# Splitting the MLP's operands into parts: three float32r products in place of one float32 product

## The chip, the core and the metric

The kernel is written directly for one core of a Trainium2 chip, whose engines run their own instruction queues and wait for each other by semaphores: TensorE (PE) for products and turns (transposes), VectorE (DVE), ScalarE (ACT), GpSimd (POOL), and SyncE (SP) for transfers. PE writes to eight banks of PSUM of 128 x 512 float32 values; the other data lie in SBUF. The metric is the time of one execution on the device, in microseconds (us), as the median of three runs.

## The reference

The input has 32 batches of 128 tokens with 128 channels. Two layers follow each other:

- layer 0 is a transformer block: modulated self-attention with 16 heads, cross-attention, and an MLP,
- layer 1 is a router over three experts with an evidence step and a gate.

The change concerns layer 0's MLP alone:

```python
x_norm2 = modulate(_ln(x), shift_m, scale_m)          # layer norm, then x * (1 + scale) + shift
h = jax.nn.gelu(x_norm2 @ W_mlp1 + b_mlp1)            # 128 -> 512
h = h @ W_mlp2 + b_mlp2                               # 512 -> 128
x = x + gate_m[:, None] * h
```

## The kernel before

Tokens are worked on in 8 groups (NG) of 4 batches (GB), 512 tokens (GT) each. The program has three stages.

**Attention**, rounds -1 to 7, by a table of steps with times (`round_steps`): each step is put at a time between 0 and 32 of its round, and every engine takes its own part of the steps in that order. Round 7 holds, beside the last attention, the derived weights of the router (`derive`), POOL's splitting of the router's weights into parts (`split`), and the first steps of the MLP. Round 8 (`i == NG`) mixes the last of attention with the MLP of groups 0 to 3.

**MLP.** The steps for a group g are:
- `stats` (DVE: statistics of the tokens, L806 to L812; POOL: add of epsilon and power, L648 and L650),
- `norm` (DVE: four operations, one for each batch, L820, from SBUF to SBUF),
- `xt` (PE: the tokens are turned so that channels are on partitions, L975),
- `xt_read` (ACT: modulation while reading the bank into `m_XT`, L725),
- `first` k = 0..3 (PE: product with a quarter of W_mlp1, L939) with the gelu of it on ACT (L713, into `m_H`); for k = 2 and 3 the gelu has a step `gelu` of its own,
- `second` k = 0..3 (PE: product with a quarter of W_mlp2, summed in one bank),
- `gate` (DVE, L835, reads that bank), `turn_back` (PE turns it back, DVE adds it to X, L841).

`MLP_STEPS` is the order of one round, each step with a lag: in the round of group i the engines do `stats` and `norm` of i + 2, `xt` of i + 1, `first` of i, `second` and `gate` of i - 1, `turn_back` of i - 2. Each engine takes its steps in this order and waits by semaphores for data and for free buffers. There is one `m_XT`, so `xt_read` of i + 1 stands behind the four `first` of i. Rounds 3 and 4 are a loop on the engines, the others are written out. From round 5 on (`rest_of_groups`) steps of the router's first groups are mixed in: the norm and turn of its tokens (`r_XN`), its scores (product with `KEYS`), the evidence (`r_EV`).

**Router**, all 8 groups, from about 405 us to the end. Its seven hidden products are already made of parts: POOL makes of a float32 tensor a part "high" in float32r (add of zero, L659) and a part "low" (the float32 tensor minus high, L661), and PE sums high x high, high x low and low x high in the bank. In the profile all products of MLP and router have the line of the helper that issues them, L939, and all turns L975.

## Time and profile before

| | |
|---|---|
| time, median of 3 runs | 579.82 us (578.67 to 581.12) |
| the profiled execution's own time | 578.05 us |
| its span | 576.3 us |
| busy: PE, DVE, ACT, POOL | 540.8, 424.9, 385.2, 271.3 us |
| granted TensorE clock over the span | 0.994 |

Busy times are those of one engine over the whole span and overlap each other. PE's weight loads (PEld) run beside its products. The MLP stage proper takes about 80 us of the span.

### The profile page before, as it was taken

How to read it: one execution, taken by the hardware profiler on the slowest of the kernel's cores; microseconds unless marked ns; L12 is line 12 of the kernel's file. 1: busy time of each engine (PE TensorE's matmuls, PEld its weight loads, DVE VectorE, ACT ScalarE, POOL GpSimd, SP SyncE). 2: the span in 40 equal slices, each digit the busy share in tenths (PEclk: the TensorE clock that was granted, in tenths of full speed). 3: DMA queues.
4: the chain of work that ended last, by engine and by line, in shares of the span. 5: the costliest groups of instructions: out<-in, count | busy, mean ns of one | idle time of the engine just before them, and what ended most of it. 6: DMA issues, size and time to landing. Idle time of an engine off the chain costs nothing.

```text
span 576.3 us, 16509 instructions
## 1 busy us (share of the span) xinstructions
PE 540.8 (94%) x6175; PEld 381.4 (66%) x6177; DVE 424.9 (74%) x1255; ACT 385.2 (67%) x897; POOL 271.3 (47%) x294
## 2 busy tenths in 40 slices
PE   7988998998999999999999889988999999999995
PEld 6745665666666666666667544444788788788895
DVE  4688987878899798899787445555586786786565
ACT  6548686777878778787777744564654854854862
POOL 5638669299494878888903110124034034034000
PEclk9999999899999999999999999999999999999998
DMA  4764656254143543334400010000001001000000
GB/s 130 162 173 127 175 155 164 56 122 126 52 116 89 134 115 97 105 90 115 114 5 3 2 36 0 2 1 19 0 19 40 18 20 36 18 18 20 19 20 18
DMA packets 48716, 39.38 MB, mean 68 GB/s; under 512 B 6241, under 2 KB 48002, under 8 KB 48642
## 3 DMA queue, kind: packets, MB, share of 16 engines
q1 hardware_dynamic: 46568, 34.62, 23.1%
q10 hardware_dynamic: 2074, 3.77, 2.3%
q8 instruction: 47, 0.77, 0.6%
q14 instruction: 27, 0.22, 0.1%
HBM read 10.06 MB, written 2.10 MB: 21 GB/s over the span
## 4 chain that ended last, share of the span: by engine, by line
PE 64%; DVE 12%; POOL 7%; DMA 5%; SPq 4%; issue 4%; ACT 3%; ACTq 0%; DVEq 0%; POOLq 0%
PE PS L939 35%; PE PS L1810 6%; PE PS L1776 5%; DVE NM L1592 3%; PE PS L975 3%; PE PS L1862 3%; SPq L1324 3%; PE PS L1874 2%; DMA Qs<-MT 2%; PE PS L1794 2%; PE PS L1832 2%; DMA Ks<-Kp 2%; PE PS L1867 2%; POOL rstd L1370 1%; POOL rest L1401 1%
## 5 line engine op out<-in xcount | busy, mean ns | idle before, releaser
L1592 DVE TENSOR_REDUCE NM<-PS 128x4 f32<-128x512 f32 x256 | 163.3, 681 | 30.8 <-PE PS L1776 30.2
L1478 ACT ACTIVATE PR<-PS 128x512 f32<-128x512 f32 x256 | 140.0, 601 | 27.1 <-PE PS L1794 26.5
L1776 PEld LDWEIGHTS PS<-Ks,Qs 64*128 64x128 bf16 x1024 | 57.0, 94 | 53.9 <-DVE NM L1592 29.3
L1776 PE MATMUL PS<-Ks,Qs 64*128 64x128 bf16 x1024 | 83.2, 218 | 6.4 <-DVE NM L1592 3.7
L1794 PE MATMUL PS<-Qs,Ks 64*128 64x128 bf16 x1024 | 83.6, 218 | 3.8 <-DMA Qs<-MT 3.2
L1810 PE MATMUL PS<-PR,Va 128*32 128x128 f32 x2048 | 82.9, 280 | 0.0
L733 ACT ACTIVATE r_HID<-PS,ANC 128x128 f32<-128x128 f32 x224 | 63.4, 383 | 20.2 <-PE PS L939 20.2
L648 POOL TENSOR_TENSOR m_veps<-m_mv,m_eps 128x4 f32<-128x4 f32 x16 | 3.2, 201 | 143.2 <-DVE m_mv L812 143.2
L1794 PEld LDWEIGHTS PS<-Qs,Ks 64*128 64x128 bf16 x1024 | 57.0, 94 | 7.4 <-DMA Qs<-MT 3.7
L1810 PEld LDWEIGHTS PS<-PR,Va 128*32 128x32 f32 x2048 | 48.3, 109 | 20.2 <-ACT PR L1478 6.1
L939 PE MATMUL PS<-r_NXS,r_WNS 128*128 128x512 f32 x168 | 53.1, 424 | 0.0
L939 PE MATMUL PS<-WO,r_HID 128*128 128x128 f32 x384 | 47.7, 278 | 0.5 <-DVE r_T L914 0.5
L939 PE MATMUL PS<-r_EVS,r_US 128*128 128x512 f32 x168 | 47.6, 392 | 0.0
L939 PEld LDWEIGHTS PS<-WO,r_HID 128*128 128x128 f32 x384 | 44.6, 192 | 2.0 <-DVE r_T L914 1.7
L1862 PE MATMUL PS<-XT,W 128*128 128x512 f32 x64 | 34.9, 633 | 1.9 <-ACT XT L1514 1.4
L939 PEld LDWEIGHTS PS<-r_EVS,r_US 128*128 128x128 f32 x168 | 31.5, 188 | 7.2
L713 ACT ACTIVATE m_H<-PS,V 128x512 f32<-128x512 f32 x32 | 21.4, 695 | 20.0 <-PE PS L939 20.0
L939 PEld LDWEIGHTS PS<-r_NXS,r_WNS 128*128 128x128 f32 x168 | 29.5, 189 | 7.8 <-issue 3.4
L939 PE MATMUL PS<-m_H,W 128*128 128x512 f32 x64 | 32.0, 600 | 2.5 <-DVE YT L835 2.5
L939 PE MATMUL PS<-m_XT,W 128*128 128x512 f32 x64 | 32.1, 601 | 0.3 <-ACT m_XT L725 0.3
L659 POOL TENSOR_TENSOR r_EVS<-r_EV,zeros 128x512 fp32r<-128x512 f32 x8 | 8.3, 1040 | 48.8 <-DVE r_EV L888 48.8
L762 ACT ACTIVATE r_GTH<-r_GS 128x512 f32<-128x512 f32 x8 | 5.1, 632 | 39.0 <-DVE r_GS L907 39.0
(197 smaller groups left out, 1102.3 us busy)
## 6 DMA issues: line engine op xcount, KB each, us to landing
Qs<-Qp SPq DMA_DIRECT2D x96, 128.0 KB
Ks<-Kp SPq DMA_DIRECT2D x90, 128.0 KB
CTXG<-in_ctx SPq DMA_DIRECT2D x8, 256.0 KB, 3.8
r_CTX<-in_ctx SPq DMA_DIRECT2D x8, 256.0 KB, 2.7
out<-X SPq DMA_DIRECT2D x8, 256.0 KB, 2.3
X<-in_x SPq DMA_DIRECT2D x7, 256.0 KB, 4.4
W<-in_weights ACTq DMA_DIRECT2D x2, 855.0 KB
Qs<-MT SPq DMA_DIRECT2D x62, 8.0 KB
```

Of the source, the lines that this page charges most:

```text
L713: nc.scalar.activation(H[:, k, :], FIRST_BANK[k % 2][:, :], ACT.Gelu_apprx_tanh, bias=vec("bmlp1", k))\
L733: last = nc.scalar.activation(HID[:, k, b * P:(b + 1) * P], HIDDEN_BANK[k % 3][:, b * P:(b + 1) * P], ACT.Silu, bias=ANC[:, k, bass.ds(g * ...
L939: return nc.tensor.matmul(to, lhsT, rhs, start=start, stop=stop)
L975: last = nc.tensor.transpose(bank[:, b * P:(b + 1) * P], source(b), ident[:, :])
L1324: sp.dma_start(to, source).then_inc(stacked[k], 16)
L1478: nc.scalar.activation(PR[:, u, :], T_BANK[u % 2][:, :], ACT.Exp, scale=SCALE)\
L1592: nc.vector.tensor_reduce(out=NM[:, c.b // 2, c.second, u // 2, u % 2 * 4:u % 2 * 4 + 4, 0], in_=S_BANK[score_bank(c, u)[0]][:, :].rearran ...
L1776: last = nc.tensor.matmul(S_BANK[bank][:, j * P:(j + 1) * P], Qs[c.stack][rows, lo + j, cols], Ks[c.stack][rows, lo + j, cols], start=True ...
L1794: last = nc.tensor.matmul(T_BANK[u % 2][:, j * P:(j + 1) * P], Ks[c.stack][rows, lo + j, cols], Qs[c.stack][rows, lo + j, cols], start=Tru ...
L1810: last = nc.tensor.matmul(O_BANK[p.turn][TW * j:TW * j + TW, at:at + P], Va[c.mem][:, c.b, 4 * (u // 2) + j, u % 2 * TW // 2:u % 2 * TW // ...
L1832: last = nc.tensor.transpose(O_BANK[c.turn][:, u * P:(u + 1) * P], OTs[:, u * P:(u + 1) * P], ident[:, :])
L1862: last = nc.tensor.matmul(PS[fill_bank(name, g)][:, :], w(WEIGHT[name[0]][kind]), source(name, g)[:, :], start=True, stop=True)
```

## The change

The products of the MLP are made as the router's are.

- The weights W_mlp1 and W_mlp2 are split by POOL in round 7 into `m_W1S` and `m_W2S`, two more `split` steps between those of the router's weights.
- The turned tokens: a new step `xt_parts` on DVE takes `m_XT` (ACT still writes it) and makes the high part (a copy that rounds to float32r) and the low part (a subtract) in one of two buffers `m_XTS0` and `m_XTS1`, by the group's parity. `xt_read` therefore waits for `xt_parts` of the group before in place of its `first`, and both stand right behind `xt` in the order.
- The gelu outputs: ACT makes the high part by a copy after each gelu (it waits for that gelu), POOL the low part by a subtract, in `m_HS`.
- Each `first` and `second` is three products of parts in float32r.
- The loop of rounds 3 and 4 is written out. The new tensors lie where attention's stacks `Qs` and `Ks` were, whose place in SBUF is moved for it. Semaphores of attention are used again.

```diff
@@ round_steps, i == NG - 1
-                 + [(t, "split", "weights", k, 0) for k, t in enumerate((2.5, 6.0, 22.5, 24.5))]
+                 + [(t, "split", "weights", k, 0) for k, t in enumerate((2.5, 6.0, 9.0, 12.0, 22.5, 24.5))]
@@ MLP_STEPS
-    ("stats", 2, 0), ("xt", 1, 0),
+    ("stats", 2, 0), ("xt", 1, 0), ("xt_read", 1, 0), ("xt_parts", 1, 0),
     ("first", 0, 0), ("second", -1, 0), ("first", 0, 1), ("second", -1, 1),
-    ("turn_back", -2, 0), ("norm", 2, 0), ("first", 0, 2), ("first", 0, 3), ("xt_read", 1, 0),
+    ("turn_back", -2, 0), ("norm", 2, 0), ("first", 0, 2), ("first", 0, 3),
     ("second", -1, 2), ("gelu", 0, 2), ("second", -1, 3), ("gelu", 0, 3), ("gate", -1, 0),
@@ gpsimd_programs, mlp
+            elif name == "first" and k < 2 or name == "gelu":
+                pool.wait_ge(h_high, 4 * g + (NG + k + 1))
+                nc.gpsimd.tensor_tensor(HS[:, 1, k, :], H[:, k, :], HS[:, 0, k, :], ALU.subtract).then_inc(h_split, 1)
@@ gpsimd_programs, split_weights
+            elif k in (2, 3):
+                pool.wait_ge(shifted_done, 16 * (2 * NG - 2))
+                to, source = ((W1S, w("mlp1")), (W2S, w("mlp2")))[k - 2]
+                return split(to, source, (weights_high, k + 1), weights_split)
@@ scalar_programs, gelu
             if later(g):
-                act.wait_ge(second_done, 4 * g + (k - 3))
+                act.wait_ge(h_split, 4 * g + (NG + k - 3))
             nc.scalar.activation(H[:, k, :], FIRST_BANK[k % 2][:, :], ACT.Gelu_apprx_tanh, bias=vec("bmlp1", k))\
                 .then_inc(gelu_done, 1)
+            act.wait_ge(gelu_done, 4 * g + (k + 1))
+            if later(g):
+                act.wait_ge(second_done, 4 * g + (k - 3))
+            nc.scalar.activation(HS[:, 0, k, :], H[:, k, :], ACT.Copy).then_inc(h_high, 1)
@@ scalar_programs, xt_read
-                    act.wait_ge(first_done, 4 * g)
+                    act.wait_ge(xt_split, g + NG)
@@ vector_programs, mlp
+            elif name == "xt_parts":
+                dve.wait_ge(xt_read, g + 1)
...
+                nc.vector.tensor_copy(XTS[par][:, 0, :], XT[:, :]).then_inc(xt_high, 1)
+                dve.wait_ge(xt_high, g + (NG + 1))
+                nc.vector.tensor_tensor(XTS[par][:, 1, :], XT[:, :], XTS[par][:, 0, :], ALU.subtract).then_inc(xt_split, 1)
@@ tensor_programs, mlp
-                product(FIRST_BANK[k % 2][:, :], w("mlp1", k * P, P), XT[:, :]).then_inc(first_done, 1)
+                chunk = slice(k * P, (k + 1) * P)
+                product(FIRST_BANK[k % 2][:, :], W1S[:, 0, chunk], XTS[par][:, 0, :], True, False)
+                product(FIRST_BANK[k % 2][:, :], W1S[:, 0, chunk], XTS[par][:, 1, :], False, False)
+                product(FIRST_BANK[k % 2][:, :], W1S[:, 1, chunk], XTS[par][:, 0, :], False, True).then_inc(first_done, 1)
...
-                pe.wait_ge(gelu_done, 4 * g + (k + 1))
-                product(SECOND_BANK[:, :], w("mlp2", k * P, P), H[:, k, :], start=k == 0, stop=k == 3)\
-                    .then_inc(second_done, 1)
+                pe.wait_ge(h_split, 4 * g + (NG + k + 1))
+                chunk = slice(k * P, (k + 1) * P)
+                product(SECOND_BANK[:, :], W2S[:, 0, chunk], HS[:, 0, k, :], k == 0, False)
+                product(SECOND_BANK[:, :], W2S[:, 0, chunk], HS[:, 1, k, :], False, False)
+                product(SECOND_BANK[:, :], W2S[:, 1, chunk], HS[:, 0, k, :], False, k == 3).then_inc(second_done, 1)
```

How this stands on the engines: first DVE in round 8, from the add of group 6's cross-attention result (L1725 before, L1766 after) to the statistics of group 3. `PS3` to `PS6` are PSUM banks, `rden` and `On` belong to attention, `m_XN` is the normalised tokens. Before:

```order
L1725 TENSOR_TENSOR X<-PS6,X 128x512
L820 TENSOR_SCALAR m_XN<-X,m_mv,m_rstd 128x128 x4
L806 BN_STATS m_stat<-X 128x6 x4
L810 COPY seen2<-m_stat 128x1
L812 BN_AGGR m_mv<-m_stat 128x2 x4
L1615 RECIPROCAL rden<-PS5 128x32
L1619 TENSOR_TENSOR On<-PS5,rden 128x256
L820 TENSOR_SCALAR m_XN<-X,m_mv,m_rstd 128x128 x4
```

After:

```order
L1766 TENSOR_TENSOR X<-PS6,X 128x512
L856 CAST m_XTS0<-m_XT 128x512
L858 TENSOR_TENSOR m_XTS0<-m_XT,m_XTS0 128x512
L839 TENSOR_SCALAR m_XN<-X,m_mv,m_rstd 128x128 x4
L825 BN_STATS m_stat<-X 128x6 x4
L829 COPY seen2<-m_stat 128x1
L831 BN_AGGR m_mv<-m_stat 128x2 x4
L1654 RECIPROCAL rden<-PS5 128x32
L1658 TENSOR_TENSOR On<-PS5,rden 128x256
L856 CAST m_XTS1<-m_XT 128x512
L858 TENSOR_TENSOR m_XTS1<-m_XT,m_XTS1 128x512
L839 TENSOR_SCALAR m_XN<-X,m_mv,m_rstd 128x128 x4
```

The parts of group 0 stand ahead of the norm of group 1, those of group 1 ahead of the norm of group 2.

Then POOL, where the router's first splits are mixed in. `m_veps` and `m_rstd` are its add and power, `r_NXS` and `r_EVS` the parts of the router's tokens and evidence. Before:

```order
L648 TENSOR_TENSOR m_veps<-m_mv,m_eps 128x4
L650 TENSOR_TENSOR m_rstd<-m_veps,half 128x4
L659 TENSOR_TENSOR r_NXS0<-r_NX0,zeros 128x512
L661 TENSOR_TENSOR r_NXS0<-r_NX0,r_NXS0 128x512
L648 TENSOR_TENSOR m_veps<-m_mv,m_eps 128x4
L650 TENSOR_TENSOR m_rstd<-m_veps,half 128x4
L659 TENSOR_TENSOR r_EVS0<-r_EV0,zeros 128x512
```

After:

```order
L655 TENSOR_TENSOR m_veps<-m_mv,m_eps 128x4
L657 TENSOR_TENSOR m_rstd<-m_veps,half 128x4
L664 TENSOR_TENSOR m_HS<-m_H,m_HS 128x512 x4
L669 TENSOR_TENSOR r_NXS0<-r_NX0,zeros 128x512
L671 TENSOR_TENSOR r_NXS0<-r_NX0,r_NXS0 128x512
L664 TENSOR_TENSOR m_HS<-m_H,m_HS 128x512 x4
L655 TENSOR_TENSOR m_veps<-m_mv,m_eps 128x4
L657 TENSOR_TENSOR m_rstd<-m_veps,half 128x4
L669 TENSOR_TENSOR r_EVS0<-r_EV0,zeros 128x512
```

Four subtracts of gelu outputs stand behind the router's first power, and four more behind its first split.

## Rows read from the trace of the kernel before

**Rows 1.** Page: busy time of each engine over the span

```profile
PE 540.8 (94%) x6175; PEld 381.4 (66%) x6177; DVE 424.9 (74%) x1255; ACT 385.2 (67%) x897; POOL 271.3 (47%) x294
```

**Rows 2.** Windows: stretch, its length, engines' busy us, clock, DMA

```profile
285.00:300.00 15.00, 14.35 (x283) 10.19 (x283) 12.58 (x27) 11.11 (x23) 2.30 (x3) 1.00 0.03 9
345.00:355.00 10.00, 10.00 (x32) 4.62 (x30) 5.53 (x22) 4.74 (x9) 1.21 (x2) 1.00 0.00 0
```

**Rows 3.** Timeline, round 3: start, us, engine, line, operation, count, idle

```profile
348.73 0.66 PE L975 MATMUL PS<-ident,m_XN 128*128 128x128 f32 x4
...
353.43 1.88 PE L939 MATMUL PS<-m_XT,W 128*128 128x512 f32 x4
...
355.15 1.88 PE L939 MATMUL PS<-m_H,W 128*128 128x512 f32 x4
...
357.07 0.66 PE L975 MATMUL PS<-ident,m_XN 128*128 128x128 f32 x4
357.24 1.36 DVE L835 TENSOR_SCALAR YT<-PS,mod,gbm 128x128 f32<-128x128 f32 x4 [1.77 <-PE PS L939]
...
359.49 0.37 DVE L812 BATCH_NORM_AGGREGATE m_mv<-m_stat 128x2 f32<-128x6 f32 x4
```

**Rows 4.** Timeline of PE in the router: two trios of float32r products

```profile
430.27 0.85 PE L939 MATMUL PS<-r_NXS,r_WNS 128*128 128x512 f32 x3
430.95 0.84 PE L939 MATMUL PS<-r_EVS,r_US 128*128 128x512 f32 x3
```

**Rows 5.** Groups from 300 us: line, operation, count, busy us, mean ns, idle

```profile
L713 ACT ACTIVATE m_H<-PS,V 128x512 f32<-128x512 f32 x32 | 21.4, 695 | 20.0 <-PE PS L939 20.0
L650 POOL TENSOR_TENSOR m_rstd<-m_veps,half 128x4 f32<-128x4 f32 x16 | 16.2, 1013 | 1.3
L725 ACT ACTIVATE m_XT<-PS,mod 128x128 f32<-128x128 f32 x32 | 12.1, 461 | 11.5 <-PE PS L939 11.5
L661 POOL TENSOR_TENSOR r_NXS<-r_NX,r_NXS 128x512 fp32r<-128x512 f32 x8 | 10.1, 1269 | 0.6
L884 DVE TENSOR_TENSOR r_WN<-r_E,r_rsum 128x512 f32<-128x512 f32 x8 | 5.5, 692 | 0.3
L762 ACT ACTIVATE r_GTH<-r_GS 128x512 f32<-128x512 f32 x8 | 5.1, 632 | 39.0 <-DVE r_GS L907 39.0
```

**Rows 6.** Timeline: norm of group 0 beside POOL, norm of group 1 alone

```profile
312.45 4.25 DVE L820 TENSOR_SCALAR m_XN<-X,m_mv,m_rstd 128x128 f32<-128x128 f32 x4 [1.42 <-POOL m_rstd L650]
...
313.50 1.27 POOL L661 TENSOR_TENSOR r_US<-U,r_US 128x512 fp32r<-128x512 f32 x1
314.72 0.82 POOL L659 TENSOR_TENSOR r_US<-U,zeros 128x384 fp32r<-128x384 f32 x1
315.63 1.00 POOL L661 TENSOR_TENSOR r_US<-U,r_US 128x384 fp32r<-128x384 f32 x1
...
322.50 1.11 DVE L820 TENSOR_SCALAR m_XN<-X,m_mv,m_rstd 128x128 f32<-128x128 f32 x4 [0.82 <-PE PS L975]
```

**Rows 7.** Timeline at the start: DVE and POOL subtract at once

```profile
15.69 1.22 POOL L1405 TENSOR_TENSOR Kp<-rest,Kp 128x512 bf16<-128x512 f32 x1
...
15.93 1.53 DVE L1717 TENSOR_TENSOR Qp<-rest,Qp 128x512 bf16<-128x512 f32 x1
```

**Rows 8.** Timeline: group 0's first products, and the turn of group 3

```profile
324.23 1.96 PE L939 MATMUL PS<-m_XT,W 128*128 128x512 f32 x4 [0.33 <-ACT m_XT L725]
...
340.66 0.63 PE L975 MATMUL PS<-ident,m_XN 128*128 128x128 f32 x4 [1.76 <-ACT m_XT L725]
```

**Rows 9.** Timeline: turn 7, router's first turn, scores, copy of evidence

```profile
374.91 0.60 PE L975 MATMUL PS<-ident,m_XN 128*128 128x128 f32 x4
...
380.08 0.60 PE L975 MATMUL PS<-ident,r_XN 128*128 128x128 f32 x4
...
383.10 1.06 PE L939 MATMUL PS<-KEYS,r_NX 128*128 128x131 f32 x8
...
395.87 0.69 DVE L888 COPY r_EV<-PS 128x512 f32<-128x512 f32 x1 [2.04 <-PE PS L939]
```

More of the change, by code:

```diff
@@ L258, in round_steps @@
                  + mlp_steps(8.43, "second", 0, 3) + mlp_steps(8.44, "norm", 3) + mlp_steps(8.45, "first", 1, 2)
-                 + mlp_steps(8.46, "first", 1, 3) + mlp_steps(8.47, "xt_read", 2) + mlp_steps(8.48, "gelu", 1, 2)
+                 + mlp_steps(8.46, "first", 1, 3) + mlp_steps(8.35, "xt_read", 2) + mlp_steps(8.36, "xt_parts", 2) + mlp_steps(5.11, "xt_parts", 1) + mlp_steps(8.48, "gelu", 1, 2)
                  + mlp_steps(8.49, "gelu", 1, 3) + mlp_steps(8.5, "gate", 0))
@@ L421, in rest_of_groups @@
         router(*step)
-    with eng.Fori(3, NG - 3) as i:
-        for name, lag, k in MLP_STEPS:
-            mlp(name, i + lag, k, 0, 0)
+    for i in range(3, NG - 3):
+        for step in valid_steps(MLP_STEPS, i):
+            mlp(*step)
     lead, second = valid_steps(ROUTER_STEPS, -2), valid_steps(ROUTER_STEPS, -1)
@@ L460, in mlp_and_router @@
 def mlp_and_router(nc, stack, X, V, ctxin, w, vec, rows1, condT, mod, gbm, half, zeros, YT, ident, PS, load_w2, out,
-                   bank_filled, bank_read, max_done, exp_done, o_normed, o_stored):
+                   bank_filled, bank_read, shifted_done, max_done, exp_done, o_normed, o_stored,
+                   high_ready, low_ready):
     def sb(name, shape, dt=F32):
@@ L532, in mlp_and_router @@
     D = rb("r_D", [P, GT])
+    W1S = rb("m_W1S", [P, 2, 4 * P], F32R)
+    W2S = rb("m_W2S", [P, 2, 4 * P], F32R)
+    XTS = [rb(f"m_XTS{k}", [P, 2, GT], F32R) for k in range(2)]
+    HS = rb("m_HS", [P, 2, 4, GT], F32R)
     reused.close()
@@ L555, in mlp_and_router @@
     bank_filled["mlp_xt"], bank_read["mlp_xt"] = xt_turned, xt_read
+    xt_high, xt_split, h_high, h_split = (high_ready["k0"], low_ready["k0"], high_ready["q0"], low_ready["q0"])
     masked = sem("masked")
@@ L681, in split_weights @@
                 pool.wait_ge(load_w2, 80)
-            elif k > 1:
-                pool.wait_ge(bank_read["derive"], DERIVED.index(("u_low", "u_high")[k - 2]) + 1)
+            elif k in (2, 3):
+                pool.wait_ge(shifted_done, 16 * (2 * NG - 2))
+                to, source = ((W1S, w("mlp1")), (W2S, w("mlp2")))[k - 2]
+                return split(to, source, (weights_high, k + 1), weights_split)
+            elif k > 3:
+                pool.wait_ge(bank_read["derive"], DERIVED.index(("u_low", "u_high")[k - 4]) + 1)
             to, source = (WNS, w("e_nx", lo, hi - lo)) if k < 2 else (US, U[:, lo:hi])
@@ L828, in mlp @@
                 normalise(0, g, XN, xt_turned)
+            elif name == "xt_parts":
+                dve.wait_ge(xt_read, g + 1)
+                if g > 1:
+                    dve.wait_ge(first_done, 4 * (g - 1))
+                elif g == 1:
+                    dve.wait_ge(exp_done, 4 * NCORE)
+                else:
+                    dve.wait_ge(shifted_done, 16 * (2 * NG - 2))
+                nc.vector.tensor_copy(XTS[par][:, 0, :], XT[:, :]).then_inc(xt_high, 1)
+                dve.wait_ge(xt_high, g + (NG + 1))
+                nc.vector.tensor_tensor(XTS[par][:, 1, :], XT[:, :], XTS[par][:, 0, :], ALU.subtract).then_inc(xt_split, 1)
             elif name == "gate":
@@ L1091, in before_router @@
         def before_router():
-            pe.wait_ge(weights_split, 2 * -(-NHC * P // GT))
+            pe.wait_ge(weights_split, 2 * -(-NHC * P // GT) + 2)
             pe.wait_ge(xt_read, NG)
@@ L1196, in build_block @@
             nc, stack, X, V, ctxin, w, vec, rows1, condT, mod, gbm, half, zeros, YT, ident, PS, load_w2, out,
-            bank_filled, bank_read, max_done, exp_done, o_normed, o_stored)
+            bank_filled, bank_read, shifted_done, max_done, exp_done, o_normed, o_stored, high_ready, low_ready)
         XN = [sb(f"XN{k}", [P, GT]) for k in range(3)]
@@ L1209, in build_block @@
         rest = sb("rest", [P, 2, GT])
-        Qs = [sb(f"Qs{k}", [P, NJ, GT], BF16) for k in range(STACKS)]
-        Ks = [sb(f"Ks{k}", [P, NJ, GT], BF16) for k in range(STACKS)]
         zrow = sb("zrow", [32, GT], BF16)
@@ L1221, in build_block @@
         On = sb("On", [P, 2, 2 * P])
+        Qs, Ks = [None] * STACKS, [None] * STACKS
+        for k in (1, 0, 2):
+            Qs[k], Ks[k] = (sb(f"{what}s{k}", [P, NJ, GT], BF16) for what in "QK")
         OgT = [sb(f"OgT{k}", [P, GT]) for k in range(2)]
@@ L1373, in body @@
                     extra["split"](ev[2])
+                elif ev[:2] == ("read", "mlp_xt"):
+                    extra["mlp"]("xt_parts", 0, 0, 0, 0)
                 elif ev[:2] == ("init", "third"):
@@ L1720, in body @@
                     extra["derive"](DERIVED[ev[2]], ev[3])
+                elif ev[:2] == ("read", "mlp_xt"):
+                    extra["mlp"]("xt_parts", 0, 0, 0, 0)
                 elif name == "read" and ev[1] in ("yt_s", "yt_c"):
```

3 lines of the change are left out of this document (2 added, 1 removed).

## The prediction

> **What bounds the kernel now.** I read the page first: TensorE (PE) is busy 94% of a span of 576.3 us, ahead of VectorE (DVE, 74%), ScalarE (ACT, 67%) and GpSimd (POOL, 47%) [rows 1]. Then the windows. The MLP stage runs from about 324 us, where the first product starts [rows 8], to about 405 us. In its middle PE is busy all ten of ten microseconds at full clock, while DVE has 5.53, ACT 4.74 and POOL 1.21 [rows 2]. So PE sets the pace there, and the other three have room. Then the timeline of one round of the MLP loop, from one turn of tokens to the next: 348.73 to 357.07 us, 8.33 us [rows 3]. Two products of one kind start 1.72 us before the next two (353.43 and 355.15), so a float32 product costs 0.86 us, in two passes of 0.43 [rows 3]. A round has eight of them (6.9 us) and two turns. Three float32r products of parts take 0.68 us together: in the router, one trio starts at 430.27 and the next at 430.95 [rows 4].
>
> **What PE gains.** Each of the 64 products of the MLP goes from 0.86 to 0.69 us: 64 x 0.17 = 10.9 us, if nothing else became late. A round's PE work falls from 8.33 to about 8 x 0.69 + 2 x 0.43 + a stall of 0.2 = 6.6 us.
>
> **What the others get.** Durations: gelu 0.695 us, tokens' read 4 x 0.35 = 1.4 us, an ACT pass over 512 columns out of SBUF 0.63 us, a POOL subtract of parts 1.27 us, POOL's power 1.01 us, a DVE two-input operation of 512 columns 0.69 us [rows 5].
> ACT: 4 copies a round. Each waits for its own gelu, so a pair costs 0.70 + 0.05 + about 0.52, 1.27 us. With the read that is 6.5 us a round: just under PE's.
> POOL: 4 subtracts, which follow one another at 1.22 (313.50 to 314.72 in [rows 6]), and add and power 1.3: 6.2 us a round where it had 1.2.
> DVE: a copy of 512 columns and a subtract. No such float32 copy is in the trace: it is longer than one norm operation of 128 columns (1.11 / 4 = 0.28 [rows 6]) and no longer than the two-input operation (0.69 [rows 5]); I take 0.42, nearer the norm, which like it reads one tensor. With gate and statistics 2.62 us (357.24 to 359.86 [rows 3]), the add of the turned-back result 0.65, the norm 1.11 [rows 6] and 1.1 for the parts, DVE has 5.5 us a round.
> On busy time alone, then, all four fit in 7 us. The question is what they do to each other.
>
> **The lock.** One place in the trace has DVE normalising tokens in SBUF while POOL makes parts, with the very instructions of this change. The four DVE operations take 4.25 us; undisturbed, they take 1.11. POOL's operations ran unhindered (1.27, 0.82, 1.00), and DVE ended at 316.70, 0.07 behind the end of POOL's last [rows 6]. Piece by piece, one DVE operation slips through for each POOL operation. The same with a two-input operation at the start: POOL runs 15.69 to 16.91, and the DVE subtract, alone 0.69, takes 1.53 and ends 0.55 after POOL [rows 7]. So while POOL is busy, each DVE operation of these kinds waits for POOL's current one to end. Gate and add have PSUM as their main input; I take them as free of this (if not, at most one POOL operation each: that is part of the second rival). Before, POOL was idle in nearly all of this stage; now it isn't.
> The Trainium skill, "SBUF — State Buffer", section "SBUF: two separate sides", states this as a rule: VectorE, in a two-port mode or with two SBUF inputs, and GpSimd take one pair of ports as an exclusive lock for a whole instruction. The trace agrees: 4.25 us against 1.11. By busy time without that rule, the sum below would be the first rival's; with it, it is mine.
>
> **A round laid out** (us after a turn starts; DVE order: gate, statistics, parts, add, norm). Gate and statistics to 2.5. POOL's add and power 2.6 to 3.9. DVE copy 2.5 to 2.9 (ACT's read, 0.65 to 2.2, is done); its subtract meets the power and ends 3.9 + 0.55 = 4.4; add to 5.05. POOL's first two subtracts 3.9 to 5.1 and 5.1 to 6.35. The norm's first operation gets through at 5.2, the second at 6.4. The third POOL subtract comes only at 6.85, because ACT's third copy waits for the second product of the round before (PE done 6.1, copy to 6.75). In that gap the last two norm operations pass, to 6.95. The next turn starts at 7.0; PE was ready at 6.6. So a round takes 7.0 us, 1.3 less than before. If the last norm operation misses the gap it is 8.25, no gain. Turn 3 starts at 340.66 [rows 8] and turn 7 at 374.91 [rows 9]: four rounds, 4 x -1.3 = **-5.2 us** (ends -5.8 and -0.3).
>
> **The way in.** The tokens' parts now stand between ACT's read and the first product: copy and subtract, 1.15 us, so the product at 324.23 moves to 325.4. PE catches part of that up. DVE's queue is the larger matter: the norm of group 2 now stands behind the parts of group 1, and these behind ACT's read of group 1 and a POOL power. Laid out in the same manner, turn 2 comes at about 334.1, 1.4 later than before. From there ACT's read ends at 336.3 and its gelu and copy pairs at 337.5, 338.8, 340.0 and 341.3. POOL's add and power for group 3 stand ahead of their subtracts and wait for DVE's statistics (337.1): power to 338.5, then four subtracts without a gap to 343.4. Into that falls the norm of group 3, four operations, one let through for each POOL operation: to 343.5. Turn 3 at 343.6 and not 340.66 [rows 8]: **+2.9 us** (ends 0 and +3.5).
>
> **The round with the router's first norm.** Turn 7 is at 374.91, the turn of the router's tokens at 380.08, its scores at 383.10 [rows 9]. After the change POOL has the router's add and power (it waits for DVE's statistics, 1.2 after turn 7) ahead of four subtracts whose data are there: busy without a gap 1.3 to 7.5. DVE has gate, keys and then parts (copy through at 4.1, subtract 5.6) and the norm's four operations (6.4, 7.6, then free, 8.1). PE reaches that turn at 5.1 and stands until 8.15. Before, it came 5.17 after turn 7, and two products that stood ahead of it now stand behind it. **+3.0 us** (ends 0 and +3.5).
>
> **The end of the stage.** From the scores to the evidence copy (383.10 to 395.87 [rows 9]) shorter products and ACT's gelu, which waits for one product less, give **-0.4 us**. The last two subtracts stand in POOL's queue between the router's splits: 396.6 + 2.4 + 1.3 + 2.4 + 1.3 = 404.1, the last product then ends at 404.8: level with before. The router's loop is untouched.
>
> **Costed at nothing.** The weights' parts are four more POOL operations, 4.6 us, in a stretch where POOL has 2.30 us of 15 [rows 2]; their wait is on work of the attention round before. The cover gone, they would push the router's weights' parts, needed only at 405. The unrolled loop and the new place of the stacks in SBUF: no time; the loop's turns show no gap of their own.
>
> **Sum.** -5.2 + 2.9 + 3.0 - 0.4 = +0.3 us. The profiled execution took 578.05 us (span 576.3 and 1.75 around it), so 578.35; the median shown is 1.77 above that execution: 579.82 + 0.3 = 580.1 us.
>
> **Rivals.**
> 1. Faster: DVE slips through in the gaps between subtracts, POOL costs it little, and PE sets the round again: rounds of 6.9, -5.7 in four; the way in +1.0, the router's norm +0.5, the end -0.4: -4.6 us, 575.2. For it: POOL's subtracts wait for ACT, and so have gaps; PE's 94%. Against: [rows 6], where gaps of 0.08 let one through and not two.
> 2. Slower: DVE starves. The last norm operation misses its gap in each round, from the point on where POOL's third subtract starts within 6.7 us of the turn: rounds of 8.25, -0.3 in four; +3.5 and +3.5 for the two places, -0.4: +6.3 us, 586.1. For it: POOL is unhindered in both meetings. Against: it needs that timing in each round.
> 3. The trios don't run at 0.69 here: a trio takes what its rows have as length, 0.84 to 0.85, and PE keeps nearly its old round: -1 in four, +2.5, +2.5, 0: +4 us, 584. Against: the starts 0.68 apart in the same rows [rows 4], the lengths overlap.
>
> **Chances.** My case 0.40, rival 1 0.25, rival 2 0.28, rival 3 0.07. What a measurement of this kernel can tell from no change is about 0.5%, 2.9 us: 576.9 to 582.7. My case (577 to 583.5) gives 0.35 within, 0.04 slower, 0.01 faster; rival 1 stays faster; rival 2 and 3 give 0.30 slower and 0.05 within. Faster 0.26, within 0.40, slower 0.34. The range from rival 1's middle to rival 2's: 574.8 to 586.2; my case's own is 577 to 583.5.
>
> **What would show it.** Turn 3 near 343.6 and turn 7 near 372.6. Mean of a DVE norm operation in the MLP near 0.8 us, while its POOL neighbours stay at 1.27. Trios of MLP products 0.69 apart. PE busy in the middle of the stage down from 10.0 to about 9 of 10 us, with waits on DVE's norm. POOL from 271 to about 317 us busy, ACT up 20. Wrong if norm operations stay at 0.34 beside POOL, if rounds take under 6.8 or over 7.9, or if waits on ACT's copies lead PE's idle time.

## The result, and the profile after

The changed kernel takes 589.41 us (median, 586.07 to 590.92), beside 580.47 us (median of four runs) for the kernel before on the same chip: a ratio of 1.0159, interval 1.0106 to 1.0213. It is slower by 1.6%, and 3.2 us beyond the top of the predicted range. The profiled execution took 588.5 us (span 586.7), 10.45 us more than that of before (578.05).

The page of the changed kernel: span, busy time of the engines, and the granted clock in 40 slices.

```profile
span 586.7 us, 16679 instructions
PE 539.5 (92%) x6241; PEld 399.7 (68%) x6241; DVE 448.8 (77%) x1271; ACT 403.2 (69%) x929; POOL 319.7 (54%) x330
PEclk9989999999999999999998978988899999999999
```

Against [rows 1], POOL has 48 us more (46 foreseen), ACT 18 (20 foreseen) and DVE 24, of which the parts are 10.6 and the longer norms nearly all of the rest; PE's busy time hardly fell, though 64 products became shorter. The clock row says why in part: slices 24 to 29 (counted from 1), which hold most of the MLP stage, have a 7 and four 8s. Windows of the same columns as [rows 2]:

```profile
345.00:355.00 10.00, 9.86 (x37) 7.29 (x37) 6.63 (x23) 7.07 (x14) 5.67 (x6) 0.76 0.01 2
353.00:363.00 10.00, 7.02 (x34) 5.15 (x33) 9.28 (x21) 7.63 (x15) 9.36 (x8) 1.00 0.01 3
```

There are two sorts of stretch. In one PE looks busy because it runs at a granted clock of 0.76 on average. In the other PE works 7.02 of 10 us, while DVE (9.28) and POOL (9.36) are full. The round between turns 4 and 5 (353.19 to 362.99) is of the second sort. Its timeline in the changed kernel (start, us, engine, line, operation, count, idle), to be laid beside [rows 3]:

```profile
353.19 0.63 PE L1005 MATMUL PS<-ident,m_XN 128*128 128x128 f32 x4
...
355.86 0.43 DVE L856 CAST m_XTS<-m_XT 128x512 fp32r<-128x512 f32 x1
...
355.95 0.39 POOL L655 TENSOR_TENSOR m_veps<-m_mv,m_eps 128x4 f32<-128x4 f32 x1
...
356.32 0.69 DVE L858 TENSOR_TENSOR m_XTS<-m_XT,m_XTS 128x512 fp32r<-128x512 f32 x1
356.42 1.46 POOL L657 TENSOR_TENSOR m_rstd<-m_veps,half 128x4 f32<-128x4 f32 x1
...
357.85 5.00 POOL L664 TENSOR_TENSOR m_HS<-m_H,m_HS 128x512 fp32r<-128x512 f32 x4
358.04 4.90 DVE L839 TENSOR_SCALAR m_XN<-X,m_mv,m_rstd 128x128 f32<-128x128 f32 x4
...
359.56 0.63 ACT L733 ACTIVATE m_HS<-m_H 128x512 fp32r<-128x512 f32 x1 [0.67 <-PE PS L969]
...
362.99 0.44 PE L1005 MATMUL PS<-ident,m_XN 128*128 128x128 f32 x2 [2.84 <-DVE m_XN L839]
```

The norm's four operations take 4.90 us, where alone they take 1.11 [rows 6]: one for each POOL subtract. PE stands 2.84 us for them, and the turn of tokens starts 9.80 us after the one before. Two rows are to be read together: POOL's power (1.46 us at 356.42) began while DVE's subtract held on, and by 1.01 us, its length of before [rows 5], it should have been over 0.45 us sooner. The lock works in both directions.

Only this one of the four rounds has a norm of 4.90. The rounds from turn 3 and from turn 5 have these:

```profile
351.04 1.86 DVE L839 TENSOR_SCALAR m_XN<-X,m_mv,m_rstd 128x128 f32<-128x128 f32 x4
...
369.07 1.87 DVE L839 TENSOR_SCALAR m_XN<-X,m_mv,m_rstd 128x128 f32<-128x128 f32 x4
```

In the last round, from turn 6, it takes 2.51 us. The four rounds take 9.37, 9.80, 8.03 and 8.29 us (8.07, 8.34, 8.50 and 9.34 before). Those from turn 3 and turn 5 begin at the slow clock shown below.

The stage falls into three stretches, and most of what follows is read from them: **way in** (turn 0 to turn 3), **rounds** (turn 3 to turn 7) and **end** (turn 7 to the first product of the router's parts, `r_NXS`). All start times are PE's, of the profiled execution of each kernel.

| kernel | way in | rounds | end | sum | norm op, mean | time, ratio (interval) |
|---|---|---|---|---|---|---|
| before | 18.93 | 34.25 | 30.04 | 83.2 | 0.44 | 1 |
| after | 22.21 | 35.49 | 36.90 | 94.6 | 0.80 | 1.0159 (1.0106 to 1.0213) |
| e1_warm | 22.75 | 38.11 | 33.29 | 94.2 | 0.96 | 1.0085 (1.0049 to 1.0122) |
| e2_no_low_part | 17.14 | 29.10 | 30.53 | 76.8 | 0.44 | 0.987 (0.980 to 0.994) |
| e3_first_only | 16.36 | 31.66 | 29.55 | 77.6 | 0.44 | 0.9886 (0.9809 to 0.9964) |
| e4_second_only | 18.77 | 32.46 | 33.02 | 84.3 | 0.71 | 0.9969 (0.9929 to 1.001) |
| e5_two_op_norm | 20.96 | 31.78 | 36.45 | 89.2 | two of 1.4 | 1.0045 (1.0006 to 1.0083) |
| e6_half_subtracts | 21.65 | 31.32 | 32.08 | 85.1 | 0.71 | 0.9978 (0.9943 to 1.0013) |
| e7_before_with_subtracts | 19.09 | 33.78 | 31.87 | 84.7 | 0.64 | 0.9973 (0.9935 to 1.0012) |
| e8_norm_early | 17.20 | 35.79 | 37.95 | 90.9 | 0.88 | 1.0062 (1.0028 to 1.0096) |
| e9_mixed | 16.36 | 30.32 | 32.94 | 79.6 | 0.44 | 0.9889 (0.9835 to 0.9943) |
| e10_quarters | 19.95 | 34.21 | 32.15 | 86.3 | 0.55 | 0.9985 (0.9949 to 1.002) |
| e11_halves_two_op_norm | 21.36 | 33.34 | 32.18 | 86.9 | two of 1.15 | 0.9998 (0.9962 to 1.0034) |
| e12_halves_warm | 22.65 | 30.38 | 32.34 | 85.4 | 0.71 | 1.0032 (0.9984 to 1.008) |

From before to after the three stretches grow by 3.3, 1.2 and 6.9 us, 11.4 in all; the rest of the program gives 1.0 back. In all these executions but e9's (497.2) the span without the sum is 490 to 494.5 us, before 493.1: the weights' parts, the written-out loop and the moved stacks, which the experiments keep, cost nothing that shows. The stretches are of one execution each, the times are medians; e2 and e6 were profiled in their fastest run, e9 in its slowest.

Behind several long waits TensorE's clock fell to the lower of its two levels. The longest is ahead of turn 3, in these timeline rows of the changed kernel (against turn 3 in [rows 8]):

```profile
338.71 4.93 POOL L664 TENSOR_TENSOR m_HS<-m_H,m_HS 128x512 fp32r<-128x512 f32 x4
338.77 4.95 DVE L839 TENSOR_SCALAR m_XN<-X,m_mv,m_rstd 128x128 f32<-128x128 f32 x4 [0.90 <-POOL m_rstd L657]
...
343.82 1.09 PE L1005 MATMUL PS<-ident,m_XN 128*128 128x128 f32 x4 [4.85 <-issue]
```

And windows of it, the first two behind that wait:

```profile
343.60:350.50 6.90, 6.68 (x22) 5.43 (x23) 3.80 (x17) 3.85 (x8) 2.69 (x4) 0.55 0.00 0
350.50:353.00 2.50, 2.50 (x12) 1.85 (x10) 2.41 (x5) 1.31 (x3) 1.29 (x1) 1.00 0.00 0
363.00:367.00 4.00, 4.00 (x13) 3.28 (x14) 3.43 (x15) 2.68 (x6) 1.38 (x2) 0.57 0.00 0
387.50:391.00 3.50, 3.13 (x10) 2.70 (x11) 1.73 (x4) 0.69 (x1) 1.04 (x1) 0.54 0.00 0
...
397.50:401.50 4.00, 4.00 (x13) 3.00 (x12) 1.43 (x10) 3.56 (x6) 1.28 (x1) 0.57 0.00 0
411.00:415.00 4.00, 3.54 (x11) 2.86 (x12) 1.44 (x7) 2.48 (x10) 2.61 (x3) 0.57 0.01 2
```

A granted clock near 0.5 is 1.2 GHz, 1.00 is 2.4 GHz. The waits ahead of the third and fourth window were 2.84 us (the round above) and 3.51 us (the router's norm). It doesn't follow each long wait: in e1 PE stood 2.97 us ahead of turn 4, in e5 3.34 us ahead of turn 3, and the stretches behind them are at 1.00.

### The profile page after: what moved, and what is told of

It is laid out like the page before. It is cut to its first block, busy times and chain, and to the rows that moved or that the text cites. A ratio compares the mean times of both kernels' runs of the same rounds, so it can differ in the third digit from the quotient of the medians.

```text
span 586.7 us, 16679 instructions
## 1 busy us (share of the span) xinstructions
PE 539.5 (92%) x6241; PEld 399.7 (68%) x6241; DVE 448.8 (77%) x1271; ACT 403.2 (69%) x929; POOL 319.7 (54%) x330
## 4 chain that ended last, share of the span: by engine, by line
PE 61%; DVE 15%; POOL 8%; DMA 5%; issue 5%; SPq 4%; ACT 2%; ACTq 0%; DVEq 0%; POOLq 0%
PE PS L969 32%; PE PS L1851 6%; PE PS L1817 5%; PE PS L1903 3%; PE PS L1005 3%; SPq L1361 3%; DVE NM L1631 3%; DVE m_XN L839 2%; DMA Qs<-MT 2%; PE PS L1915 2%; PE PS L1835 2%; PE PS L1873 2%; PE PS L1908 2%; DMA Ks<-Kp 1%; POOL rstd L1407 1%
## 5 line engine op out<-in xcount | busy, mean ns | idle before, releaser
L1851 PE MATMUL PS<-PR,Va 128*32 128x128 f32 x2048 | 83.2, 281 | 0.0
L655 POOL TENSOR_TENSOR m_veps<-m_mv,m_eps 128x4 f32<-128x4 f32 x16 | 3.9, 241 | 94.9 <-DVE m_mv L831 94.6
L664 POOL TENSOR_TENSOR m_HS<-m_H,m_HS 128x512 fp32r<-128x512 f32 x32 | 41.1, 1301 | 20.1 <-ACT m_HS L733 20.1
L969 PE MATMUL PS<-m_HS,m_W2S 128*128 128x512 f32 x96 | 31.0, 448 | 5.0 <-DVE YT L865 4.9
L969 PE MATMUL PS<-m_XTS,m_W1S 128*128 128x512 f32 x96 | 31.6, 455 | 1.5 <-DVE m_XTS L858 1.5
```

What stands on the lines that cost most here:

```text
L664: nc.gpsimd.tensor_tensor(HS[:, 1, k, :], H[:, k, :], HS[:, 0, k, :], ALU.subtract).then_inc(h_split, 1)
L969: return nc.tensor.matmul(to, lhsT, rhs, start=start, stop=stop)
L1851: last = nc.tensor.matmul(O_BANK[p.turn][TW * j:TW * j + TW, at:at + P], Va[c.mem][:, c.b, 4 * (u // 2) + j, u % 2 * TW // 2:u % 2 * TW // ...
```

## The experiments

**Theory A**: POOL's subtracts of the gelu parts lock DVE's norm. **Theory B**: the slow clock behind the waits makes the loss. **Theory C**: the copies and subtracts lengthen the chain from gelu to product, and that makes the loss. All runs are of the changed kernel with the edit shown, except where it says so. The expectations put in below use the letters a little otherwise: A takes in all that follows from the lock, e1's B is the lock alone, with the clock's fall hidden, and C also takes in the parts on DVE.

**1. Clock.** Unused products fill PE's idle time ahead of four places.

```diff
+STACKS = 3; SPARE_TURN = {3: 17, 5: 10}
+                if g in SPARE_TURN:
+                    spare_products(PS[7], SPARE_TURN[g])   # W1S x W1S, result unused
                 pe.wait_ge(d_norm[0], g + 1)
```

> The changed kernel, with idle-time products on PE (float32r, 512 columns, into a bank that nobody reads) in front of the waits at which PE stood longest: 17 before turn 3, 10 before turn 5, 12 before the turn of the router's first tokens, 8 before the first second-product of group 6. Each lot is about as long as the wait it stands in. Theory A (lock, and the clock's fall behind each wait as a cost of its own): the waits on DVE's norm end where they did (turn 3 near 343.8), but the 3.4 us stretches at half clock behind them go, and the time falls by 3 to 6 us from 589, to 583 to 586. Theory B (lock alone, the clock's fall is hidden since PE has room): 588 to 590.

Measured: 586.79 us, 1.0085, 2.6 us less than after, between the two spans given, and the intervals of e1 and after overlap. The clock rose to 0.987 from 0.976, yet the rounds got longer, not shorter: 38.11 us for four. One of its rounds, the norm and what follows it:

```profile
358.30 5.05 POOL L665 TENSOR_TENSOR m_HS<-m_H,m_HS 128x512 fp32r<-128x512 f32 x4
358.58 4.85 DVE L840 TENSOR_SCALAR m_XN<-X,m_mv,m_rstd 128x128 f32<-128x128 f32 x4
...
363.49 0.66 PE L1006 MATMUL PS<-ident,m_XN 128*128 128x128 f32 x4 [0.54 <-DVE m_XN L840]
```

In the changed kernel the rounds from turn 3 and from turn 5 began at half clock; ACT's copies came further apart, POOL had gaps, and the norm got through in 1.86 and 1.87 us. In e1 the three rounds that begin at full clock all meet the backlog (norms of 4.81 to 4.85 us) and take 9.4 to 9.8 us. The fourth begins at 0.57, behind a wait of 2.77 us; its norm takes 1.87 and the round 9.36. So in the rounds the slow clock and the lock cover one another.

Behind the rounds the clock has a price of its own. The router's turn and scores in e1, at a clock of 1.00:

```profile
390.38 0.66 PE L1006 MATMUL PS<-ident,r_XN 128*128 128x128 f32 x4 [0.82 <-DVE r_XN L840]
...
393.64 1.07 PE L970 MATMUL PS<-KEYS,r_NX 128*128 128x131 f32 x8
```

They are 3.26 us apart here and 4.55 in the changed kernel, and the whole end is 3.6 us shorter. In e1 this is nearly spent again in the longer rounds and the way in: 94.2 us for the stage, 94.6 in the changed kernel.

**2. No POOL subtracts.**

```diff
-                pool.wait_ge(h_high, 4 * g + (NG + k + 1))
-                nc.gpsimd.tensor_tensor(HS[:, 1, k, :], H[:, k, :], HS[:, 0, k, :], ALU.subtract).then_inc(h_split, 1)
-                product(SECOND_BANK[:, :], W2S[:, 0, chunk], HS[:, 1, k, :], False, False)
+                product(SECOND_BANK[:, :], W2S[:, 0, chunk], HS[:, 0, k, :], False, False)
```

> The changed kernel with POOL's subtracts of the gelu outputs left out; the second of the three second-products takes the high part again, so that PE's work is the same (the low part of the gelu outputs is left out of the result). Theory A (POOL's subtracts keep DVE's norms waiting, and all else follows from it): norm operations are back at 0.34 us, turn 3 comes at about 340, rounds are 6.7 to 7.0 us, the clock stays full, time 568 to 573. Theory C (the added passes on ACT and DVE and the longer chains of waits cost the time, POOL's part is small): 582 to 588.

Measured: 572.07 us, 0.987: 17 us below the changed kernel, as A had it. Rounds of 6.80, 7.00 and 6.99, then 8.31 for the one with the router's keys. ACT's copies and DVE's parts are all still there, so they aren't the main cause. The chain from gelu to product is shorter by the subtract too; whether that makes the gain is left to experiment 6. One round of this run, DVE and POOL:

```profile
347.29 0.69 DVE L855 TENSOR_TENSOR m_XTS<-m_XT,m_XTS 128x512 fp32r<-128x512 f32 x1
347.39 1.46 POOL L657 TENSOR_TENSOR m_rstd<-m_veps,half 128x4 f32<-128x4 f32 x1
348.38 0.69 DVE L868 TENSOR_TENSOR X<-PS,X 128x512 f32<-128x512 f32 x1 [0.40 <-PE PS L1002]
348.99 1.11 DVE L836 TENSOR_SCALAR m_XN<-X,m_mv,m_rstd 128x128 f32<-128x128 f32 x4
```

The norm is back at 1.11. The power is at 1.46 here too, with no other POOL work about: DVE's subtract alone stretches it by 0.45.

**3 and 4. One half of the change at a time.** First product in parts, second in float32 from `m_H` (no copy, no POOL subtract); and the reverse, where the first product and the place of its steps are as before.

```diff
# e3
-                product(SECOND_BANK[:, :], W2S[:, 0, chunk], HS[:, 0, k, :], k == 0, False)   (and its two fellows)
+                product(SECOND_BANK[:, :], w("mlp2", k * P, P), H[:, k, :], start=k == 0, stop=k == 3)
# e4
-                product(FIRST_BANK[k % 2][:, :], W1S[:, 0, chunk], XTS[par][:, 0, :], True, False)   (and its two fellows)
+                product(FIRST_BANK[k % 2][:, :], w("mlp1", k * P, P), XT[:, :])
```

> Only the first product is made of parts (tokens' parts on DVE as in the changed kernel); second products, gelu and H as before, no copies on ACT and no subtracts on POOL. Theory A: 32 products save 0.17 us each, 5.4 us, DVE's parts cost about 1 on the way in: 575 to 577, norm operations at 0.34 us. Theory C: DVE's parts in front of the norms cost as much as they bring: 580 to 583.

> Only the second product is made of parts (gelu copies on ACT, subtracts on POOL); first products, m_XT and the place of its read as before, no tokens' parts on DVE. Theory A: the norms meet the subtracts as in the changed kernel, so most of the loss is here: 584 to 588, with norm operations of 0.7 to 1.2 us. Theory C (DVE's own parts make the loss, by their length and place): 576 to 580.

Measured: 573.09 us (0.9886) and 578.72 us (0.9969). The first half alone is 1.1% faster than before, with nothing more on POOL in a round; A gave 575 to 577, so it came out better still. The second half alone makes no difference that its interval can tell; A in its plain form expected 584 or more and missed, and the time lies in C's span. Its norm operations are slowed (0.71), though less than in the changed kernel: in three of its four rounds the norm takes 2.74 to 3.02 us and meets two subtracts in a row, where 4.90 met four. And its float32 products leave the round more time. So the lock by itself doesn't make the loss; which of the two, the shorter backlog or the longer round, spares e4 is not separated.

**5. Norm as two operations of 512 columns** with two inputs each, instead of four of 128.

```diff
-            for b in range(GB):
-                last = nc.vector.tensor_scalar(to[:, b * P:(b + 1) * P], x_batch(g, b), mv[...], rstd[...], ALU.subtract, ALU.mult)
+            nc.vector.tensor_tensor(view, x, mv[:, s, :, 0:1].to_broadcast([P, GB, P]), ALU.subtract)
+            nc.vector.tensor_tensor(view, view, rstd[:, s, :].unsqueeze(2).to_broadcast([P, GB, P]), ALU.mult)
```

> The changed kernel with each token norm of MLP and router made of two two-input operations over 512 columns (minus mean, times deviation, operands spread by broadcast) in place of four single-input operations over 128 columns. Alone they take longer (2 x 0.69 against 1.11). Theory A (one DVE operation is let through for each POOL operation, so the number of operations counts): norms beside POOL fall from 4.9 to about 2.5 to 3.1 us, turn 3 comes near 342, time 581 to 585. If DVE were held up in proportion to its own work and not by the piece, it would be 589 to 592.

Measured: 584.09 us, 1.0045; inside what A gave. Two such operations are 1.38 us at 0.69 each [rows 5], where the four took 1.11; the rounds are shorter all the same (31.78 against 35.49), because the norm needs two ways through and not four. The price is on the other side, in these groups of the run (busy us, mean ns):

```profile
L664 POOL TENSOR_TENSOR m_HS<-m_H,m_HS 128x512 fp32r<-128x512 f32 x32 | 45.7, 1450 | 14.7 <-ACT m_HS L733 14.7
L842 DVE TENSOR_TENSOR m_XN<-m_XN,m_rstd 128x512 f32<-128x512 f32 x8 | 12.2, 1530 | 0.3
L839 DVE TENSOR_TENSOR m_XN<-X,m_mv 128x512 f32<-128x512 f32 x8 | 10.3, 1281 | 2.5 <-POOL m_rstd L657 2.5
```

POOL's subtract went from 1301 to 1450 ns: it waits for DVE too.

**6. Each subtract in two of 256 columns.**

```diff
-                nc.gpsimd.tensor_tensor(HS[:, 1, k, :], H[:, k, :], HS[:, 0, k, :], ALU.subtract).then_inc(h_split, 1)
+                nc.gpsimd.tensor_tensor(HS[:, 1, k, 0:h], H[:, k, 0:h], HS[:, 0, k, 0:h], ALU.subtract)
+                nc.gpsimd.tensor_tensor(HS[:, 1, k, h:GT], H[:, k, h:GT], HS[:, 0, k, h:GT], ALU.subtract).then_inc(h_split, 1)
```

> The changed kernel with each POOL subtract of the gelu outputs in two operations of 256 columns. POOL's work grows by a start each (about 0.15 to 0.2 us, 5 us in all). Theory A (DVE waits for POOL's current operation to end, so shorter ones let it through sooner): norms beside POOL fall from 4.9 to about 3 us, time 583 to 587. If only POOL's total busy time counts: 590 to 593.

Measured: 579.8 us, 0.9978, better than the 583 to 587 expected: no loss is left that the interval can tell, with the same arithmetic on the same engines. The chain from gelu to product is no shorter than in the changed kernel, so this, with e2, puts out C as well. A round of the run:

```profile
354.20 0.74 POOL L665 TENSOR_TENSOR m_HS<-m_H,m_HS 128x256 fp32r<-128x256 f32 x1
354.90 0.73 POOL L666 TENSOR_TENSOR m_HS<-m_H,m_HS 128x256 fp32r<-128x256 f32 x1
...
354.32 2.77 DVE L842 TENSOR_SCALAR m_XN<-X,m_mv,m_rstd 128x128 f32<-128x128 f32 x4
```

Four norm operations pass in 2.77 us, four POOL operations at 0.70 apart: one way through for each operation, whatever its length. POOL's total hardly rises (324.5 us against 319.7).

**7. The kernel before with POOL made busy**: a subtract of weights into an unused buffer behind each gelu, its products float32.

```diff
+                pool.wait_ge(gelu_done, 4 * g + (k + 1))
+                nc.gpsimd.tensor_tensor(HS[:, 1, k, :], w("mlp1"), w("mlp2"), ALU.subtract)   # unused
```

> The kernel before (float32 products, tokens' read in its old place, no copies on ACT, no parts on DVE) with one POOL subtract of 512 columns after each gelu, of two weight tensors into a buffer that nobody reads. No engine waits for it but POOL itself and whom POOL keeps waiting. Theory A: norm operations of the MLP rise from 0.34 to about 0.8 us and more, the time by 2 to 6 us to 582.5 to 586.5. Theory C (the loss is in the longer chains on ACT and DVE): 580 to 581.

Measured: 580.01 us, 0.9973: no loss, a miss for A, and at C's span of 580 to 581. Norm operations rose to 0.64 us and the rounds stayed at 33.78. This round shows the cover:

```profile
355.15 2.21 DVE L835 TENSOR_SCALAR m_XN<-X,m_mv,m_rstd 128x128 f32<-128x128 f32 x4
...
357.98 0.63 PE L1001 MATMUL PS<-ident,m_XN 128*128 128x128 f32 x4
```

The norm ends at 357.36 and its turn is due at 357.98, behind float32 products. Here too the subtracts come in twos, and the norm takes 2.2 us, not 4.90. With e4 it says: contention costs nothing as long as the norm ends before PE is ready for its turn.

**8. Norm earlier**: the statistics a round sooner, and the norm ahead of the parts in DVE's order. The steps of the way in are moved likewise, which is not shown.

```diff
-    ("stats", 2, 0), ("xt", 1, 0), ("xt_read", 1, 0), ("xt_parts", 1, 0),
+    ("xt", 1, 0), ("xt_read", 1, 0), ("norm", 2, 0), ("xt_parts", 1, 0),
-    ("turn_back", -2, 0), ("norm", 2, 0), ("first", 0, 2), ("first", 0, 3),
+    ("stats", 3, 0) (behind the first "second"), ("turn_back", -2, 0), ("first", 0, 2), ("first", 0, 3),
```

> The changed kernel with the same instructions in another order: statistics (and POOL's add and power) three groups ahead in place of two, so that a norm stands at a round's start, when its deviation is there and before POOL's subtracts of that round; parts after it; likewise for groups 3 and 4 on the way in. Theory A: turn 3 comes near 339.5, rounds take 6.9 to 7.5 us, the stall at the router's first norm stays (about 4 us): 574 to 579, below the kernel before. If the lock's cost only moves to other operations (parts, power): 583 to 588.

Measured: 585.75 us, 1.0062: a miss for A's 574 to 579, and inside the span given for a cost that only moves. The way in is 17.20 us, with turn 3 at 338.58, near where it was expected (339.5). The rounds are not: 10.23, 7.00, 10.09 and 8.47. Of this run:

```profile
349.63 5.03 POOL L664 TENSOR_TENSOR m_HS<-m_H,m_HS 128x512 fp32r<-128x512 f32 x4
...
350.29 4.46 DVE L839 TENSOR_SCALAR m_XN<-X,m_mv,m_rstd 128x128 f32<-128x128 f32 x4
...
358.97 0.51 PE L969 MATMUL PS<-m_HS,m_W2S 128*128 128x512 f32 x1 [1.86 <-DVE YT L865]
```

The norm meets the backlog here too (4.04 to 4.67 us in each round), and now holds up the parts and the gate behind it, for which PE waits 1.86 us. Moving the victim in its queue moved the loss; it did not remove it.

**9. Second product half in parts**: chunks 0 and 1 of each group in float32, 2 and 3 in parts, so that POOL's two subtracts come late in a round.

```diff
-            elif name == "first" and k < 2 or name == "gelu":
-                pool.wait_ge(h_high, 4 * g + (NG + k + 1))
+            elif name == "gelu":
+                pool.wait_ge(h_high, 2 * g + (NG + k - 1))
```

> The changed kernel, but the second product's first two chunks of each group are float32 products again, without copy or subtract of the parts; its last two chunks and the whole first product stay in parts. POOL then has two 1.3 us subtracts a round, both of them behind the gelus 2 and 3, late in the round. If the loss comes from four subtracts queued back to back when the norm's operations start (theory A with the backlog), the norm operations fall near 0.45 to 0.6 us each, rounds 3 to 7 are at 7.1 to 7.5 us, and the time is 571 to 575. If what costs is the late chunks' wait (copy and subtract between gelu 3 and the last product, on the way to the gate), rounds stay over 8 us and the time is 578 to 583.

Measured: 573.64 us, 0.9889. Rounds of 6.96, 7.37, 7.34 and 8.65, norm operations 0.44 us. Of this run, one round:

```profile
350.44 2.51 POOL L664 TENSOR_TENSOR m_HS<-m_H,m_HS 128x512 fp32r<-128x512 f32 x2 [2.86 <-ACT m_HS L738]
...
353.58 1.46 POOL L657 TENSOR_TENSOR m_rstd<-m_veps,half 128x4 f32<-128x4 f32 x1
...
355.54 1.11 DVE L844 TENSOR_SCALAR m_XN<-X,m_mv,m_rstd 128x128 f32<-128x128 f32 x4
```

POOL's subtracts fall beside gate and statistics (350.4 to 353), POOL is idle at 355.04 to 357.80, and the norm runs there alone. The time is inside what the backlog gave (571 to 575). The subtracts are also half as many, so the run can't tell their number from their time; that the norm is at 1.11 us with POOL idle beside it is what it shows. Rounds are faster than in e3 by 1.3 us; the end of this profiled run is slow by its clock (0.73 and 0.70 in 385 to 391), so no more than the tie of e3 and e9 can be said: both beat both kernels.

**10 to 12. Remedies deepened or joined.** Quarters of 128 columns; halves with the two-operation norm; halves with the spare products of e1.

```diff
# e10
+                for q in range(4): ... tensor_tensor(HS[:, 1, k, c], H[:, k, c], HS[:, 0, k, c], ALU.subtract)   # c = 128 columns
# e11 = e6 + e5, e12 = e6 + e1
```

> The changed kernel with each POOL subtract in four operations of 128 columns instead of one of 512. If one VectorE norm operation is let through per POOL operation, smaller operations give it more ways through: norm operations 0.55 to 0.65 us each (0.71 with halves), time 577 to 581. If POOL's own issue time per operation decides instead, the four cost POOL over 1.6 us a chunk, the second product's wait grows, and the time is 582 to 588.

> Both earlier remedies together: POOL's subtracts in two operations of 256 columns, and the norm as two two-input operations of 512 columns. If the lock between the engines goes both ways and by operation, the two remedies overlap: with short POOL operations the four short norm operations already get through, and the two long ones delay POOL more. Then 580 to 584, no better than the halves alone (579.8). If the two add, 574 to 577.

> The halved subtracts with spare TensorE products in its idle time (17 before turn 3, 10 before turn 5, 12 before the router's norm turn, 8 before the second product of group 6; results unused). If TensorE's half clock behind its waits still costs once the lock is nearly gone, the mean granted clock rises to 0.987 or more and the time falls to 576 to 578.5. If the clock matters only as a follower of the lock's waits, 579 to 582: the spare products may even delay what they are in front of, by up to 0.3 us each place.

Measured: 579.81 us (0.9985), 579.33 (0.9998) and 582.17 (1.0032, interval 0.9984 to 1.008). Quarters bring the norm down to 0.55 us an operation, but POOL now spends 57.6 us on them where halves took 47.4: no gain over halves. The two remedies don't add. And with the lock eased, the spare products give nothing: e12's profiled run has a clock of 0.990, e6's without them 0.996. e10 came as its first branch had it; e11 and e12 were in kind as their branches of no gain said, each within 0.7 us of the span given.

## Why the prediction was wrong, by its own steps

**What PE gains, and what the others get.** Right. Trios of products start 0.69 apart at full clock, DVE's copy takes 0.43 us alone (0.42 taken), POOL gained 48 us (46 foreseen), and rival 3 is out.

**The lock.** Right in kind, and gate and add are free of it, as it took them to be. Wrong in one point: POOL's operations "ran unhindered". In the place shown there they did; beside DVE's two-input subtract they don't. Power 1.46 for 1.01 (after, e2, e3, e9), subtracts 1.45 for 1.30 (e5), while in e7 and e8, where no DVE subtract falls beside it, the power keeps 1.01. The case with a two-input operation [rows 7] was read only for what it did to DVE. The Trainium skill, "SBUF — State Buffer", section "SBUF: two separate sides", has it that whichever of the two starts first keeps the pair for its whole instruction and the other "fully blocks"; the rows agree in both directions (4.90 us for 1.11, and 1.46 for 1.01), and only one of the two had been carried into the layout.

**A round laid out: the step that failed.** -5.2 us foreseen, +1.2 measured: 6.4 us, more than the other terms miss by together. The gap from 6.35 to 6.85, in which the last two norm operations were to pass, is not there when PE runs at full clock. In the round from turn 4 POOL's first subtract starts 4.66 us behind the turn and not at 3.9; 0.45 of these 0.76 us is the stretched power. Two subtracts end near 7.2, and ACT's third copy is done at 7.00 (360.19), so POOL goes on without a gap, and the two operations pass behind the third and the fourth subtract: 9.80 for the 7.0 foreseen. In e1's three rounds at full clock the first subtract starts at 4.20 to 4.35, two are over at 6.7 to 6.9 and the third copy is done at 6.6 to 6.9: there the power's 0.45 us alone takes up nearly all of the 0.5 us that the gap was to have. This is the second rival's mechanism, "the last norm operation misses its gap", but its price was capped at a round of 8.25: it lets one operation miss where two do.

In the rounds from turns 3 and 5 the gap came back, and the norm (1.86 and 1.87) took the 1.9 us of the layout. They are long, 9.37 and 8.03, because they begin at half clock behind waits of 4.85 and 2.84 us that the lock made. Without POOL's subtracts PE was to be ready at 6.6 and rival 1 had rounds of 6.9; e2 has 6.8 to 7.0. The mean of a norm operation, foreseen near 0.8, is 0.80, but that is no sign for the layout: it is a mean over norms of 1.11 to 4.95 us, and the 4.90 of the round above is one that the layout had at 1.9.

**The way in.** +2.9 foreseen, +3.2 by turn 3 (343.82; 343.6 foreseen), with the product at 325.28 (325.4). Right in mechanism and size. In e8 the same stretch is 5 us shorter by the order alone.

**The round with the router's first norm.** +3.0 foreseen, +4.9 measured (8.19 us from turn 7 to the scores before [rows 9], 13.11 after). The lock's part is right: POOL's four subtracts took 5.61 us and DVE's parts 2.80 beside them, and in e1, at full clock, turn and scores come 7.97 and 11.23 us behind turn 7, which is +3.0. These rows of the changed kernel carry it:

```profile
381.61 5.61 POOL L664 TENSOR_TENSOR m_HS<-m_H,m_HS 128x512 fp32r<-128x512 f32 x4
...
382.05 1.14 DVE L856 CAST m_XTS<-m_XT 128x512 fp32r<-128x512 f32 x1
383.22 1.66 DVE L858 TENSOR_TENSOR m_XTS<-m_XT,m_XTS 128x512 fp32r<-128x512 f32 x1
384.81 3.01 DVE L839 TENSOR_SCALAR r_XN<-X,m_mv,m_rstd 128x128 f32<-128x128 f32 x4
```

The turn came 8.56 us behind turn 7, where 8.15 was foreseen; from there to the scores it is 4.55 us, at a clock of 0.54 in most of it, where e1 has 3.26 at 1.00: 1.3 us of the term are the clock's.

**The end.** -0.4 foreseen, about +1.9 measured: +0.5 from scores to the evidence copy, +1.4 from there to the first `r_NXS` product. Two more slow stretches lie in it (a clock of 0.57 in 397.5 to 401.5 and in 411 to 415). But for the clock the layout was right: in e5, with POOL's four subtracts a group as in the changed kernel and a clock of 1.00, it is 21.64 us from the scores to that product, 0.2 less than before (21.85). The last piece is level, as foreseen, where the clock is full: from the router's second turn to that product 8.24 us before, 8.21 in e1, 8.22 in e4 and e5 (only e10, with its quarters on POOL, has 8.84). It is 9.67 in the changed kernel, and 10.07 in e7 and 9.35 in e2, which has no such subtracts, each with a stretch of 5 to 6 us at 0.67 to 0.71. So it is the slow clock, and not POOL's subtracts, that lengthens it. Two float32 products there, in the kernel before and then in e7:

```profile
401.38 1.98 PE L939 MATMUL PS<-m_H,W 128*128 128x512 f32 x4 [0.84 <-DVE YT L835]
...
402.13 3.58 PE L965 MATMUL PS<-m_H,W 128*128 128x512 f32 x4 [1.07 <-DVE YT L861]
```

**Not considered at all.** TensorE's clock. Behind the new waits of 4.85, 2.84 and 3.51 us stand stretches at 0.54 to 0.57 of full clock. In the rounds it takes the place of the lock's waits and costs little beyond them (e1). In the router's round and the end it costs about 3 us, by the comparisons with e1 and e5; an estimate without them, 589.4 less 3, is still at the top of the range and not near 580.1. In e6's profiled execution, where the lock is eased, the clock is 0.996 with no spare products. The range lacked both: two operations missing the gap, and a price for the clock. The range's own ends, 574.8 and 586.2, are also not quite the middles of its rivals, 575.2 and 586.1.
